# A graph network with an eigenvector stage: z's term as a one-row product on TensorE, the tangents' sum on GpSimd, the basis copy on ScalarE, and the reflection's scalars ahead of the copy of Y

## The chip, the cores and the metric

One NeuronCore of a Trainium2 chip runs the whole program in one launch. The metric is the device time of an execution in microseconds. Engines: TensorE (PE in the profile, its weight loads PEld), VectorE (DVE), ScalarE (ACT), GpSimd (POOL) and SyncE (SP), each with its own in-order queue; they meet at semaphores only.

## The reference

The input is x, 64 x 128 x 128 in float32, and a sparse matrix `adj`, 128 x 128. Four layers follow, each as `x = layernorm(x + layer(x))`: layer 0 a graph convolution with two batch norms, layer 2 graph attention over 256 edges with four heads, layer 3 two graph convolutions and then windowed LSTMs of 1 to 4 steps. The one that matters here is layer 1:

```
deg = sum(A, 0) + sum(A, 1) - diag(A)
L_norm = d_inv_sqrt[:, None] * (diag(deg) - A) * d_inv_sqrt[None, :]
_, U = eigh(L_norm)
agg = einsum('mn,bnd->bmd', U.T, features)
h = relu(agg @ W1 + b1);  out = h @ W2 + b2
return einsum('nm,bmd->bnd', U, out)
```

All eigenvectors of a 128 x 128 matrix are needed, with their signs fixed, before layer 1 can begin.

## The kernel before, in words

The program is written out without loops on the chip; every engine's queue is written by its own function, in its own order. After the loads and the graph's matrices (to 39 us of the span) comes the eigenvector stage (39 to about 458 us), and then layers 1, 2 and 3 and the final norm.

In the eigenvector stage three things run interleaved.

- *Sixteen Jacobi turns* (`SWEEPS`) that improve a basis V of eigenvectors, kept as it is (`v_nat`) and transposed (`v_t`). A turn, in the order of its chain: W = L V on TensorE (`pe_w`, L507), copied by ScalarE (L1069); the off-diagonal products (`pe_off`, L511, L512) and the diagonals (GpSimd's product L1406, then `pe_diagonals`, L516, L517); VectorE's differences (L1626); ScalarE's square, sign and absolute value (L1077 to L1079); the sum (L1631) and its root on ScalarE (`act_hyp`, L1083); the tangents on VectorE (`dve_tangents`: sum L1637, reciprocal L1638, product L1639); a norm on ScalarE (L1087 to L1089) and the scaled B on VectorE (L1643 to L1645); B transposed (L521); X (L1649); Y and the first product with V (L525 to L527); the copy of Y on ScalarE (`act_y`, L1094); Y squared (L531, L532) and its copies (L1098, L1099); the polynomial on VectorE (L1653 to L1664) with one more product (L537); and the new V and V transposed (`pe_v`, L542, L543), copied by VectorE (`dve_v`, L1669) and ScalarE (`act_vt`, L1104). In turns 9, 11, 13 and 15 (`POLISHED`) a correction of V with three more products and a second pair of copies follows.
- *Sixty-three reflection steps* that bring the matrix to tridiagonal form, one column each (what they keep fixes the signs of the eigenvectors at the end); four steps go with a turn and a fifth with a polished one (`steps_of`), none with turn 8, where the first 32 are put together to a basis (`removal_turn`). A step: VectorE computes the next column as a row c (L1713) and its sum of squares (L1720); ScalarE scales and takes a root (`act_vector`, L1115, L1117); GpSimd makes the scalars (`pool_scalars`: sign L1390, live L1392, sigma L1394, the changed leading entry L1397, half the square L1399). Meanwhile TensorE has made the matrix of the step before (L571, L573, L574 into `h_mat`), ScalarE copies it (`act_matrix`, L1124, L1125), TensorE multiplies out a row of it and y (`pe_rows`, L562, L563) and ScalarE copies the row (`act_row`, L1132). VectorE then forms z = sigma * row + y (L1689), the reciprocal (L1691), v scaled (L1692, which SyncE stores with a small DMA), a reduction of their product (L1696), w (L1698), a helper row (L1702) and the next c. w and v scaled go to TensorE for the rank-two change (`pe_rank`).
- *Layer 0 as side work* (`beside`, `behind_rank`): the slot number is the reflection step. Steps 0 to 20 carry the aggregation (L460) and hidden products (L467, saved by ScalarE, L1003), 22 to 40 the output products (L473, L474) and their statistics, 43 to 63 the transposition back (L481), the addition (L1578), the layer-norm statistics (L1581, L1585) and the writing of x.

`jacobi_turn(i)` exists once for each engine and lists these pieces by hand: four steps h0 to h3 and the turn's operations between them. Each engine waits where it stands, so a piece that is not ready holds all that is listed behind it.

## Time and profile before

| what | value |
|---|---|
| median of three runs | 1087.52 us (1086.25 to 1088.42) |
| the profiled execution | 1086.33 us, span 1084.5 us |
| TensorE busy in the span | 933.4 us (86%), 4093 instructions |
| VectorE busy | 659.7 us (61%), 2237 instructions |
| ScalarE busy | 569.2 us (52%), 1460 instructions |
| GpSimd busy | 158.8 us (15%), 390 instructions |
| mean granted TensorE clock | 0.881 |

The span is what the profiler saw from the first to the last instruction; the execution's own time is 1.8 us longer. Busy shares are means over stages with different limits. The chain of waits (the work that ended last, followed back) is what tells for a stretch which engine was late. A piece of it is the part of an instruction that lies on the chain, so it can be shorter than the instruction.

### The profile page before, as it was taken

To read this page: it belongs to the slowest core of one execution; us is meant where nothing else is said; L and a number is where in the kernel's file an instruction comes from. 1 tells how busy PE (TensorE), PEld (TensorE's weight loads), DVE (VectorE), ACT (ScalarE), POOL (GpSimd) and SP (SyncE) were. 2 spreads that over 40 slices of the span, in tenths; PEclk is the share of its full clock that TensorE was granted. 3 is DMA by queue.
4 is the path that set the end of the run, shared out by engine and by line. 5 is a ranking of instruction groups with operands and counts; after the bars stand their busy time and mean duration, and the time that the engine had idled before them with its cause. 6 is when DMAs were issued, how large, how long until landed. Compare 5 with 4: busy or idle time off the path is not lost.

```text
span 1084.5 us, 13522 instructions
## 1 busy us (share of the span) xinstructions
PE 933.4 (86%) x4093; PEld 631.0 (58%) x4093; DVE 659.7 (61%) x2237; ACT 569.2 (52%) x1460; POOL 158.8 (15%) x390
## 2 busy tenths in 40 slices
PE   4788867878866676699999999999999998899995
PEld 3555545545555565466788877886444465554443
DVE  4667676654757788357635598533544455553686
ACT  0555543754534665338655345534965565664456
POOL 0122222311322222100000000000011111110055
PEclk9699985977956555589999999999999999999998
DMA  9100000000000000000000000000000000000014
GB/s 261 32 1 1 1 1 0 1 1 1 1 1 1 1 1 1 1 1 1 1 1 1 1 2 1 2 1 1 1 1 0 0 1 1 1 0 1 0 40 116
DMA packets 14328, 12.99 MB, mean 12 GB/s; under 512 B 897, under 2 KB 11057, under 8 KB 14257
## 3 DMA queue, kind: packets, MB, share of 16 engines
q1 hardware_dynamic: 14018, 11.98, 3.9%
q8 instruction: 33, 0.54, 0.2%
q14 instruction: 39, 0.31, 0.1%
q10 hardware_dynamic: 238, 0.16, 0.1%
HBM read 7.89 MB, written 4.19 MB: 11 GB/s over the span
## 4 chain that ended last, share of the span: by engine, by line
PE 71%; DVE 18%; ACT 5%; issue 3%; POOL 1%; DMA 0%; DVEq 0%; SPq 0%; POOLq 0%; ACTq 0%
PE bank L884 15%; PE bank L908 9%; PE bank L805 3%; PE bank L750 3%; PE bank L740 3%; PE bank L764 3%; PE bank L795 3%; PE bank L467 2%; PE bank L573 2%; PE bank L704 2%; PE bank L460 1%; PE bank L715 1%; PE bank L871 1%; PE bank L813 1%; PE bank L863 1%
## 5 line engine op out<-in xcount | busy, mean ns | idle before, releaser
L1330 ACT ACTIVATE hid_t<-bank,gate_b 128x512 f32<-128x512 f32 (+1 forms) x252 | 150.8, 631 | 67.8 <-PE bank L908 66.7
L908 PE MATMUL bank<-ms,w_t 128*128 128x512 f32 (+1 forms) x288 | 112.9, 536 | 6.8 <-DVE ms L2062 6.8
L884 PE MATMUL bank<-hid_t,w_t 128*128 128x336 f32 (+1 forms) x296 | 106.4, 506 | 1.1 <-DVE x L2066 1.1
L1422 POOL COPY hid_t<-feat_t 128x1008 f32<-128x1008 f32 (+1 forms) x12 | 27.9, 2328 | 499.3 <-DVE feat_t L2058 499.3
L884 PE MATMUL bank<-feat_t,w_t 128*128 128x512 f32 x208 | 93.1, 603 | 0.0
L908 PEld LDWEIGHTS bank<-ms,w_t 128*128 128x128 f32 x288 | 54.6, 193 | 56.5 <-issue 34.3
L884 PEld LDWEIGHTS bank<-hid_t,w_t 128*128 128x128 f32 x296 | 56.2, 191 | 46.0 <-issue 26.2
L1124 ACT ACTIVATE hs<-bank,con 128x1 f32<-128x1 f32 x62 | 16.2, 261 | 102.3 <-PE bank L574 102.3
L1337 ACT ACTIVATE hid_t<-hid_t 128x512 f32<-128x512 f32 (+1 forms) x72 | 41.8, 580 | 52.3 <-DVE hid_t L2044 27.6
L884 PEld LDWEIGHTS bank<-feat_t,w_t 128*128 128x128 f32 x208 | 39.2, 189 | 50.9 <-issue 46.7
L982 ACT ACTIVATE x<-x,perm 128x128 f32<-128x128 f32 x128 | 52.3, 482 | 2.6 <-DVE perm L1461 2.6
L2044 DVE TENSOR_TENSOR hid_t<-hid_t 128x512 f32<-128x512 f32 (+1 forms) x36 | 42.3, 1175 | 17.0 <-ACT hid_t L1330 16.9
L467 PE MATMUL bank<-at,w_t 128*128 128x512 f32 x64 | 36.2, 649 | 15.1 <-ACT hid_t L1003 15.1
L2047 DVE TENSOR_TENSOR hid_t<-hid_t 128x512 f32<-128x512 f32 (+1 forms) x36 | 21.9, 609 | 42.5 <-ACT hid_t L1330 42.5
L1891 DVE TENSOR_TENSOR ht<-ht,bank 128x512 f32<-128x512 f32 x32 | 21.9, 688 | 40.4 <-ACT ht L1258 40.4
L2058 DVE TENSOR_TENSOR feat_t<-hid_t 128x512 f32<-128x512 f32 (+1 forms) x36 | 25.9, 720 | 26.4 <-ACT hid_t L1337 26.4
L1429 POOL TENSOR_SCALAR x<-x,perm 128x128 f32<-128x128 f32 x32 | 29.3, 928 | 75.8 <-DVE perm L2091 75.8
L562 PE MATMUL bank<-u_t,con 128*1 128x127 f32 (+62 forms) x126 | 24.6, 286 | 17.7 <-ACT u_t L1125 10.8
L2062 DVE TENSOR_TENSOR ms<-hid_t 128x512 f32<-128x512 f32 (+1 forms) x36 | 22.0, 611 | 25.2 <-ACT hid_t L1337 25.2
L2049 DVE TENSOR_TENSOR hid_t<-hid_t 128x512 f32<-128x512 f32 (+1 forms) x36 | 21.9, 610 | 24.9 <-ACT hid_t L1330 24.9
L1258 ACT ACTIVATE ht<-bank 128x512 f32<-128x512 f32 x32 | 19.1, 597 | 33.6 <-PE bank L750 33.6
L1394 POOL TENSOR_SCALAR hs<-hs 1x1 f32<-1x1 f32 x64 | 21.5, 336 | 88.6 <-ACT hs L1117 88.4
(443 smaller groups left out, 2166.7 us busy)
## 6 DMA issues: line engine op xcount, KB each, us to landing
out<-x SPq DMA_DIRECT2D x16, 256.0 KB, 2.6
con<-in_constants SPq DMA_DIRECT2D x1, 449.0 KB, 3.2
hid_t<-in_L_gnn_W SPq DMA_DIRECT2D x2, 128.0 KB, 3.7
e_int<-in_L_gnn_src ACTq DMA_DIRECT2D x1, 128.0 KB
l_w<-in_L_gnn_W SPq DMA_DIRECT2D x2, 64.0 KB
wg<-in_L_gnn_Wg SPq DMA_DIRECT2D x2, 64.0 KB
adj_n<-in_adj SPq DMA_DIRECT2D x1, 64.0 KB, 3.7
hid_t<-in_L_gnn_W_lin SPq DMA_DIRECT2D x1, 64.0 KB, 3.3
```

Of the source, the lines that this page charges most:

```text
L467: mm(l0_mid[k][:, :], w_t[:, WB_W1 + k, :], at[n % 2][:, :, :], start=True, stop=True).then_inc(s["l0_hid"], 1)
L740: d = mm(bank[2 + k][:, b * E:(b + 1) * E], xs[t % 2][:, 2 * k + b, :], w_t[:, WB_LIN:WB_LIN + 2, :], start=True, stop=True)
L750: d = mm(bank[4 + k][:, b * E:(b + 1) * E], z_lin[t % 2][:, 2 * k + b, :], sum_st[:, :], start=True, stop=True)
L764: d = mm(bank[6 + half][:, 0:E], head_strip[:, P - HEADS - r:2 * P - HEADS - r], rhs[:, b * E:(b + 1) * E], start=(r == 0), stop=(r == P - ...
L795: mm(bank[2 * (t % 2) + c][:, :], dst_st[:, c * P:(c + 1) * P], z_val[:, t * TB:(t + 1) * TB, :], start=True, stop=True).then_inc(s["l2v_v ...
L805: d = mm(bank[4][:, b * P:(b + 1) * P], w[c][:, b, :], src_s[:, c, :], start=(c == 0), stop=(c == EC - 1))
L884: return mm(bank[4 * u + BANK_OF[g]][:, 0:w], w_t[:, WB_IH + 4 * (it.p - 1) + g, :], lstm_x(n), start=True, stop=(it.k == 0))
L908: mm(bank[4 * u + BANK_OF[g]][:, 0:w], w_t[:, WB_HH + 4 * (it.p - 1) + g, :], lstm_h_of(it.chain)[:, 0:w], start=False, stop=True).then_in ...
L982: d = f(x[:, t * TB + b, :], x[:, t * TB + b, :], ACT.Identity, scale=ln_rs[:, t, b:b + 1], bias=ln_shift[:, t, b:b + 1])
L1330: f(dst[:, 0:w], bank[4 * u + BANK_OF[g]][:, 0:w], ACT.Tanh if g == G_G else ACT.Sigmoid, bias=gate_b[:, 4 * (it.p - 1) + g:4 * (it.p - 1) ...
L1337: f(th[n % 4][:, 0:w], cc[it.chain % 2][:, 0:w], ACT.Tanh).then_inc(s["lstm_tanh"], 1)
L2044: tt(c[:, 0:w], gi[u][:, 0:w], gg[u][:, 0:w], ALU.mult).then_inc(s["lstm_c"], 1)
```

## The change

Four edits in the eigenvector stage, and a renaming.

- z's term: the product y now stays open in its bank (`stop=False`), and a new function `pe_z(h)` adds sigma times the row by a product of one row with a 1x1 weight. It waits for the row (`h_a_row`) and for sigma (`h_sigma`) and signals `h_rows`. VectorE's L1689 is gone; the reduction and w read the bank directly. `pe_z` stands ahead of `beside` in each step: behind W in step 0, behind the transposition of B in step 2, behind Y squared in step 3.
- The tangents' sum: `jabs + jhyp` is now done by GpSimd (`pool_den`) behind the scalars of the turn's second step; VectorE waits for `j_den`.
- The basis copy: the copy of V into `v_nat` moves from VectorE (`dve_v`) to ScalarE, inside `act_vt`, ahead of the copy of V transposed.
- Scalars: in step 2 ScalarE runs `act_vector` ahead of `act_y` and no longer behind it.
- The semaphores `fin_var`, `fin_std` and `fin_scale` are replaced by counts on `ln_var`, `ln_std` and `ln_scale`; the waits stay the same.

```diff
-                mm(h_y[:, k:P], c_col, a_sb[:, k:P], start=True, stop=True).then_inc(s["h_rows"], 1)
+                mm(h_y[:, k:P], c_col, a_sb[:, k:P], start=True, stop=False)
+
+            def pe_z(h):
+                if h is None or h == HALF - 1:
+                    return
+                k = h + 1
+                pe.wait_ge(s["h_a_row"], h + 1)
+                pe.wait_ge(s["h_sigma"], h + 1)
+                mm(h_y[:, k:P], scalar(h, SIGMA), a_row[h % 2][:, k:P], start=False, stop=True).then_inc(s["h_rows"], 1)
...
                 pe_rows(h0)
                 pe_w(i)
+                pe_z(h0)
                 beside(h0)
                 pe_off(i)
                 pe_rank(h0)
                 pe_diagonals(i)
                 behind_rank(h0)
                 pe_rows(h1)
+                pe_z(h1)
                 beside(h1)
                 pe_rank(h1)
                 behind_rank(h1)
                 pe_rows(h2)
                 pe_turn(i)
+                pe_z(h2)
                 beside(h2)
                 pe_rank(h2)
                 pe_y(i)
                 behind_rank(h2)
                 pe_rows(h3)
                 pe_y2(i)
+                pe_z(h3)
                 beside(h3)
                 pe_f(i)
...
+                act.wait_ge(s["j_v"], i + before + polished + 1)
+                t = f(v_nat, j_v, ACT.Copy)
+                if polished or i not in POLISHED:
+                    t.then_inc(s["j_v_sb"], 1)
+                else:
+                    t.then_inc(s["j_m"], 1)
                 act.wait_ge(s["j_vt"]
...
                 act_row(h2)
                 beside(h2)
-                act_matrix(h2)
+                act_step(h2)
                 act_y(i)
-                if h2 is not None:
-                    act_vector(h2 + 1)
...
+            def pool_den(i):
+                pool.wait_ge(s["j_hyp"], i + 1)
+                pool.tensor_tensor(jt, jabs, jhyp, ALU.add).then_inc(s["j_den"], 1)
+
             pool_scalars(0)
             for i in range(SWEEPS):
                 pool_vw(i)
-                for h in steps_of(i):
+                for n, h in enumerate(steps_of(i)):
+                    if n == 1:
+                        pool_den(i)
                     if h is not None and h != STEPS_BEFORE - 1 and h + 1 < HALF:
                         pool_scalars(h + 1)
...
             def dve_tangents(i):
-                dve.wait_ge(s["j_hyp"], i + 1)
-                link(tt(jt, jabs, jhyp, ALU.add))
+                dve.wait_ge(s["j_den"], i + 1)
                 link(dve.reciprocal(jhyp, jt))
                 tt(jt, jos, jhyp, ALU.mult).then_inc(s["j_t"], 1)
...
                 if h < HALF - 1:
-                    dve.wait_ge(s["h_rows"], h + 1)
                     dve.wait_ge(s["h_a_row"], h + 1)
-                    dve.wait_ge(s["h_sigma"], h + 1)
-                    link(stt(z_row[:, k:P], a_row[h % 2][:, k:P], scalar(h, SIGMA), h_y[:, k:P], ALU.mult, ALU.add))
                 dve.wait_ge(s["h_half"], h + 1)
                 link(dve.reciprocal(scalar(h, INV), scalar(h, HALFSQ)))
                 ts(pv[:, k:P], v[:, k:P], scalar(h, INV), None, ALU.mult).then_inc(s["h_pv"], 1)
                 if h == HALF - 1:
                     return
                 dve.wait_ge(s["h_pv"], h + 1)
-                link(dve.tensor_tensor_reduce(e_vec[:, k:P], pv[:, k:P], z_row[:, k:P], 0.5, 0.0, ALU.mult, ALU.add,
+                dve.wait_ge(s["h_rows"], h + 1)
+                link(dve.tensor_tensor_reduce(e_vec[:, k:P], pv[:, k:P], h_y[:, k:P], 0.5, 0.0, ALU.mult, ALU.add,
                                               hs[0:1, 16:17]))
-                stt(w_row[:, k:P], v[:, k:P], hs[0:1, 16:17], z_row[:, k:P], ALU.mult, ALU.subtract).then_inc(s["h_w"], 1)
+                stt(w_row[:, k:P], v[:, k:P], hs[0:1, 16:17], h_y[:, k:P], ALU.mult, ALU.subtract).then_inc(s["h_w"], 1)
...
-                dve_v(i, 0)
```

## Rows read from the trace of the kernel before

**Rows 1.** The page's slices of 27.1 us each, granted clock; windows: busy us by engine, PEclk, DMA share, GB/s

```profile
PEclk9699985977956555589999999999999999999998
...
400.00:440.00 40.00, 26.66 (x120) 22.17 (x120) 30.96 (x159) 22.62 (x88) 9.11 (x33) 0.54 0.00 1
```

**Rows 2.** Sources by line: ns min/median/max, first and last start, forms

```profile
L563 PE MATMUL bank<-u_t,hs x126: 229/269/420, 39.4 to 435.5; 128*1 128x127 f32 x2, 128*1 128x126 f32 x2, 128*1 128x125 f32 x2, 128*1 128x124 f32 x2
...
L1637 DVE TENSOR_TENSOR perm<-perm x16: 271/273/291, 49.0 to 426.3; 128x128 f32<-128x128 f32 x16
...
L1669 DVE COPY av<-bank x20: 260/284/292, 64.5 to 443.3; 128x128 f32<-128x128 f32 x20
...
L1689 DVE SCALAR_TENSOR_TENSOR rows<-rows,hs,bank x63: 262/298/335, 40.0 to 437.6; 1x127 f32<-1x127 f32 x1, 1x126 f32<-1x126 f32 x1, 1x125 f32<-1x125 f32 x1, 1x124 f32<-1x124 f32 x1
```

**Rows 3.** Chain of waits in the stage: start us, us, what; first and last pieces

```profile
39.58 0.42 PE bank L563 x2
...
148.47 0.23 DVE rows L1689
...
150.19 0.21 DVE perm L1637
...
426.34 0.21 DVE perm L1637
...
435.56 0.21 PE bank L563 x2
...
437.60 0.28 DVE rows L1689
```

**Rows 4.** Instructions in order of time: start us, us; the end of turn 14

```profile
415.51 0.28 ACT L1104 ACTIVATE av<-bank 128x128 f32<-128x128 f32 x1 [0.37 <-PE bank L543]
...
416.44 0.28 DVE L1669 COPY av<-bank 128x128 f32<-128x128 f32 x1
...
416.78 0.80 PE L507 MATMUL bank<-av,lap 128*128 128x128 f32 x2 [0.77 <-DVE av L1669]
```

**Rows 5.** Instructions in order of time, step 3 of turn 14

```profile
411.84 0.27 DVE L1689 SCALAR_TENSOR_TENSOR rows<-rows,hs,bank 1x69 f32<-1x69 f32 x1
...
413.20 0.69 PE L573 MATMUL bank<-rows,src_st 1*128 1x69 f32 x2 [0.43 <-DVE rows L1698]
```

**Rows 6.** Instructions in order of time, step 1 of turn 6

```profile
195.43 1.12 PE L473 MATMUL bank<-ht,w_t 128*128 128x512 f32 x2
...
195.98 0.23 ACT L1132 ACTIVATE rows<-bank 1x102 f32<-1x102 f32 x1
...
198.02 0.46 PE L573 MATMUL bank<-rows,seg 1*128 1x102 f32 x2 [0.41 <-DVE rows L1698]
```

**Rows 7.** Instructions in order of time, step 3 of turn 6

```profile
208.46 0.30 DVE L1660 SCALAR_TENSOR_TENSOR diag_mat<-perm,diag_mat 128x128 f32<-128x128 f32 x1
...
209.29 0.15 DVE L1691 RECIPROCAL hs<-hs 1x1 f32<-1x1 f32 x1 [0.19 <-POOL hs L1399]
```

**Rows 8.** Instructions in order of time, step 1 of turn 3

```profile
124.93 1.10 PE L467 MATMUL bank<-at,w_t 128*128 128x512 f32 x2 [1.39 <-ACT hid_t L1003]
```

**Rows 9.** Instructions in order of time, step 1 of turn 0

```profile
46.67 2.08 PE L460 MATMUL bank<-ahat_t,x 128*128 128x128 f32 x8
...
46.85 0.25 ACT L1132 ACTIVATE rows<-bank 1x126 f32<-1x126 f32 x1
```

**Rows 10.** Instructions in order of time, step 0 of turn 14

```profile
391.75 0.45 POOL L1406 TENSOR_TENSOR wv<-av,wv 128x128 f32<-128x128 f32 x1 [1.51 <-ACT wv L1069]
...
391.77 0.52 DVE L1702 SCALAR_TENSOR_TENSOR rows<-rows,tmp 1x71 f32<-1x71 f32 x1
```

**Rows 11.** Instructions in order of time, step 2 of turn 14

```profile
404.83 0.28 DVE L1645 TENSOR_SCALAR src_b<-perm,js 128x128 f32<-128x128 f32 x1
...
406.38 0.28 DVE L1702 SCALAR_TENSOR_TENSOR rows<-rows,seg 1x69 f32<-1x69 f32 x1
...
406.59 0.33 DVE L1649 TENSOR_SCALAR src_b<-bank,js 128x128 f32<-128x128 f32 x1
```

## The prediction: what the change does to the time

> **What bounds the kernel now.** I read the table of slices on the page first, then the busy times of a stretch, then the chain of waits through the eigenvector stage, and last the instructions in order of time, turn by turn. The change touches only the stage from 39 to about 458 us; what comes after has TensorE at full speed and nearly always busy, and the edits there only rename semaphores. In the slices the reader is to see TensorE's granted clock: 0.5 to 0.9 in most slices of the stage, 0.9 and 1.0 after it; from 400 to 440 us it is 0.54, so mostly the lower level of 1.2 GHz, with TensorE busy 26.7 of 40 us and VectorE 31.0 [rows 1]. No engine is full there. The stage is two recurrences, the reflections (63 steps) and the Jacobi turns (16), on five in-order queues, with layer 0 as side work, and what counts is which queue is late at each step.
>
> The chain says it by place. The old term of z (L1689 on VectorE) is on it at 16 of 63 steps, the tangents' sum (L1637) at 12 of 16 turns, the copy of V (L1669) 8 times of 20; the product beside them, L563 on TensorE, is on it at 23 steps [rows 3]. So VectorE is late in the quiet turn 4 and from 350 us on, where the layer-0 additions and statistics are on it; TensorE, or ScalarE in front of it, is late in turns 0 to 3 and at the long side products of turns 5 to 10.
>
> **z's term moved to TensorE.** Removed: one VectorE instruction of 0.298 us median [rows 2] and its link wait of some 0.03. Where it is on the chain it gives its piece: 16 pieces from 148.47 to 437.60 us [rows 3] sum to 4.4 us, with the links 4.9. Added: a product with a 1x1 weight and one row of at most 127 columns, two passes as every float32 product here. The trace has no such operation. The nearest row is L563, as many columns with 128 rows under them: on the chain it takes 0.42 at the lower clock with 127 columns and 0.21 near the end with 65 [rows 3]. The upper bound is L573, one row under 128 weight columns, 0.69 for both passes with its restart [rows 5]; the lower is nothing, where TensorE idles anyway. I take 0.25 for the place in the queue and 0.45 until VectorE can read. VectorE needs z only at the reduction, some 0.5 us after the reciprocal, so where row and sigma are early the product is covered, and where it is not, VectorE waits 0.1 to 0.2.
>
> It costs in the TensorE queue. It is put ahead of the side work, and it waits for the row (ScalarE, L1132) and for sigma; side work, rank products and diagonals stand behind it.
> - At step 0 of a turn it follows W, at step 3 Y squared. In turns 1 to 3 ScalarE covers it: TensorE idles 1.39 us before the hidden product, waiting for a saved tile [rows 8]. Of the 23 places where L563 is on the chain I count 8 so covered; the other 15 cost 0.25 each, 3.8 us.
> - At step 2 it stands between the transposition of B and the side work, both on the chain at 7 turns: 1.8 us.
> - At step 1 the row is late, as ScalarE makes it behind the three operations on the differences. In turn 6 the side product L473 starts at 195.43, while the row is done at 196.21, so it starts at 196.5 instead. L573 started at 198.02 after 0.41 us of idling for w [rows 6]; 1.05 later it starts about 0.65 late, ScalarE's next matrix with it, and what VectorE saved in this step is lost. The same holds in turns 7, 9 and 10: four times 0.5, 2.0 us. In turn 0 L460 starts at 46.67 and the row ends at 47.10 [rows 9]: 0.43 of waiting and the product, 0.8 us, all on the chain.
>
> VectorE now reads the bank twice. Same form, same size class: L1689, which reads a bank, took 0.27, L1702 from SBUF alone 0.28 [rows 5, 11]; L1649, from a bank, 0.33, where L1645, from SBUF, took 0.28 [rows 11]. So between -0.01 and +0.05 an instruction; I take 0, by the row of the same form, and keep 0.05.
>
> The Trainium skill says otherwise, in "VectorE: DVE Perf Modes", section "The TRN2 errata": a VectorE operation from PSUM has 120 fixed cycles where one from SBUF has 58. At the page's 0.96 GHz that would be 0.065 us an instruction, 0.13 a step, by my estimate some 8 us over 62 steps if all were on the chain; L1689 against L1702 does not agree with it.
>
> **Tangents' sum to GpSimd.** L1637 takes 0.273 us, 16 times [rows 2]; 12 pieces from 150.19 to 426.34 us [rows 3] sum to 2.6, with links 3.0. GpSimd needs about 0.45, as for L1406, same size and type [rows 10]. It waits for the root, behind it are only the scalars of the next step, which have nothing to do yet. The reflection's five VectorE instructions (over 1.2 us) cover it except in turn 8, which has none: there 0.45 and two semaphores replace 0.3, a loss of 0.2. While L1406 ran, L1702 took 0.52 for its usual 0.28 [rows 10, 11], so 0.24 can come back at each turn; its lower end is 0, as the reciprocal that now runs beside the sum has one input. I take 0.1 a turn: gain 3.0 - 1.2 - 0.2 = 1.6 us.
>
> **Copy of V to ScalarE, ahead of that of V transposed.** The 8 pieces of the chain, from 164.78 to 416.44 us (the last one's instruction is in [rows 4]), sum to 1.9 us, with restarts 2.2. At the ends of the late turns there is more: in turn 14 V transposed is copied at 415.51, but V only at 416.44, behind the statistics, and W's product starts at 416.78 after 0.77 us idle [rows 4]. With both on ScalarE, each 0.25 to 0.28 and overlapping by some 0.1, W starts near 416.05: 0.7 gained, so 0.4 beyond the copy, at four such ends, 1.6. Sum 3.8 us. ScalarE pays 0.2 ahead of the row of the next step; where W came at once anyhow (turn 6) W is 0.1 later, which I leave inside the rounding.
>
> **Scalars ahead of the copy of Y.** On ScalarE square and root of the next step ran behind the copy of Y, and in turn 6 the reciprocal waited for GpSimd until 209.29, with L1660 done at 208.76 [rows 7]. Now L1660 ends last: 0.5 us, in turn 6 and likewise turn 9, 1.0 us. Elsewhere VectorE's own order is later. The copy of Y is not delayed: it waits for three products behind the rank, longer than the scalars take.
>
> **Sum.** Gains 4.9 + 1.6 + 3.8 + 1.0 = 11.3; costs 3.8 + 1.8 + 2.0 + 0.8 = 8.4; net -2.9 us. The profiled execution took 1086.33 us (span 1084.5), which gives 1083.4; the median of the three runs is 1.2 us above it, so 1084.6 on that footing. By stretch: turn 0 about +1, turns 1 to 3 none, turn 4 about -1, turns 5 to 10 none, turns 11 to 15 about -3.
>
> **Rivals.**
> - *TensorE's queue decides (slower).* Place: the new product ahead of the side work. Price: 0.25 each, 62 times, 15.5 us, and holds of 2.8. It decides from the point where more than (11.3 - 2.8) / 0.25 = 34 products are on the path instead of the 22 counted. For it: 23 steps have L563 on the chain, and removing VectorE work makes TensorE the later one. Against: TensorE idles 0.4 to 0.8 us ahead of W and of the rank products [rows 4, 5]. With 45 on the path: +2.8, 1090.3. Chance 0.16.
> - *Hidden on both sides.* Each engine relieved was late by less than the next one: in turn 14 L573 had idled only 0.43 us for w [rows 5], and the product z takes 0.25 of it. If half of the gains are so cut: -5.6 + 5.6 (the costs that lie on the same steps shrink too), 1087.5. Chance 0.18.
> - *The bank read costs.* VectorE holds a bank longer than SBUF at each read: 0.05 twice a step at the 31 or so steps where VectorE is late, +3.1, 1087.6. L1649 speaks for it, L1689 against it [rows 5, 11]. Chance 0.05. (The skill's page on VectorE, section "The TRN2 errata", would price these same steps at 4 us, an estimate.)
> - *The holds cost nothing and the late turns give fully.* Without the 2.0 of turns 6 to 10 and the 1.8 at step 2: -6.7, 1080.8. For it: VectorE was last there too, so half of the delay is slack. Chance 0.13.
> - *The clock moves.* Between turns 4 and 11 the granted clock changes often [rows 1]; an L473 to L474 stretch costs twice as much at the lower level. Shifted turns can meet another level at one or two places, 1 to 2 us either way, the sign open. This widens every case and has no chance of its own.
>
> **Numbers.** My forecast, a gain of 1.5 to 5 us, has 0.48. It is likeliest at 1084.5. Its own range is 1082.2 to 1086.0; from 1080.3 to 1089.5 about 2 in 10 are left out. 0.2% is 2.2 us, about what a measurement of this kernel can tell from no change; faster means under 1085.3. Faster: 0.40 of the forecast's 0.48, the 0.13, and 0.03 of the hidden case: 0.56. Slower: the first rival and a little of the third: 0.18. Same: 0.26.
>
> **What would show it.** VectorE: no L1689, and the reciprocal straight behind L1660 or behind GpSimd's last scalar; a wait of VectorE for TensorE ahead of the reduction under 0.2 us at most steps. If that wait is over 0.4, the term of z is mis-sized. TensorE: the new product some 0.2 us in the queue at the upper level and 0.3 at the lower; L460 in turn 0 some 0.8 later against L563's end, L473 of step 1 in turn 6 some 1 us. W's product in turn 14 within 0.3 us of the copy of V transposed. The distance between successive matrices of differences (L1626) shorter by 0.5 to 1 us from turn 11 on and unchanged in turns 1 to 3. It is wrong if turns 1 to 3 grow, or if turns 11 to 15 shrink by less than 1.5 us together, or if the stage's granted clock moves by more than 0.03.

## The result: 1090.45 us, slower by 0.44%

| | before | changed |
|---|---|---|
| median, us | 1086.8 (1085.38 to 1088.53, 20 executions) | 1090.45 (1086.5 to 1101.04, 20 executions) |
| ratio | | 1.0044 (1.003 to 1.0059) |
| profiled execution / its span, us | 1086.33 / 1084.5 | 1091.17 / 1089.1 |
| granted clock of the profiled execution | 0.881 | 0.877 |

I had forecast 1084.5, and 0.56 for faster. The time lies outside the wider of my two ranges (1080.3 to 1089.5) by 1 us, and on the other side of the kernel before. One execution of `no_z` below took 1963 us: it stands apart from all others, and its range, ratio and low time leave it out, while its median of five counts it.

In the changed kernel the lines are: L563 and L564 the row products, L572 the new one-row product, L580, L582 and L583 the rank products, L1152 the row on ScalarE, L1118 and L1124 the copies of V and of V transposed, L1702 the reciprocal, L1708 the reduction, L1714 the last of the reflection's vectors; the side work is L461, L474, L475, L482. The clock slices of the profile after and one of its windows, in the form of [rows 1]:

```profile
PEclk9599985895956555589999999999999999999998
...
400.00:440.00 40.00, 28.60 (x128) 22.12 (x128) 29.93 (x156) 23.03 (x89) 10.42 (x35) 0.50 0.01 1
```

TensorE is busy 28.6 of 40 us where it was 26.7, VectorE 29.9 where it was 31.0: work moved, but the time did not fall. The distances between the matrices of differences (L1626 before, L1650 after) say where. After the start of turn 0 they give: turn 0 +3.3 us, turns 1 to 4 +0.4, turns 5 to 10 +4.4, turns 11 to 15 -3.4. The late turns are as forecast (-3), turn 0 (+1) and turns 5 to 10 (none) are not. The 4.4 hide more: turn 7 alone is 3.6 us shorter (18.1 for 21.7), and TensorE's lower level is gone from it (0 us for 10.2); the five others grew by 8.1.

The new product's line, with what TensorE idled for ahead of it and who waited for it:

```profile
L572 PE MATMUL bank<-rows,hs x126: 226/262/415, 39.4 to 441.5; 1*1 1x127 f32 x2, 1*1 1x126 f32 x2, 1*1 1x125 f32 x2, 1*1 1x124 f32 x2
its engine sat idle before it (us, times) until:
  ACT rows L1152: 21.5, 30
...
  POOL hs L1412: 0.9, 2
who waited for it (us, times):
  DVE rows L1708: 5.8, 13
```

So at 30 of 63 steps TensorE stands still for the row, 21.5 us in all, where I had named five. In the chain of waits (start, us, what) L572 now has 36 pieces, which sum to 12.2 us; the first and the last:

```profile
39.49 0.51 PE bank L572 x2
...
436.09 0.32 PE bank L572 x2
```

I had counted 22 places at 0.25, 5.6 us. VectorE's L1708 has no more than 5.8 us of waiting for it in all.

### The profile page after: what moved, and what is told of

It reads as the page before. It is cut to its first block, busy times and chain, and to the rows that moved or that the text cites. A ratio compares the mean times of both kernels' runs of the same rounds, so it can differ in the third digit from the quotient of the medians.

```text
span 1089.1 us, 13759 instructions
## 1 busy us (share of the span) xinstructions
PE 962.8 (88%) x4219; PEld 639.7 (59%) x4219; DVE 632.1 (58%) x2138; ACT 572.5 (53%) x1480; POOL 165.3 (15%) x406
## 4 chain that ended last, share of the span: by engine, by line
PE 76%; DVE 14%; ACT 6%; issue 3%; POOL 1%; ACTq 0%; DMA 0%; DVEq 0%; POOLq 0%
PE bank L898 15%; PE bank L922 9%; PE bank L582 3%; PE bank L819 3%; PE bank L754 3%; PE bank L764 3%; PE bank L778 3%; PE bank L809 3%; PE bank L468 2%; PE bank L461 2%; PE bank L583 2%; PE bank L474 2%; PE bank L718 1%; PE bank L729 1%; PE bank L475 1%
## 5 line engine op out<-in xcount | busy, mean ns | idle before, releaser
L2056 DVE TENSOR_TENSOR hid_t<-hid_t 128x512 f32<-128x512 f32 (+1 forms) x36 | 21.9, 609 | 42.2 <-ACT hid_t L1348 42.2
L468 PE MATMUL bank<-at,w_t 128*128 128x512 f32 x64 | 36.7, 656 | 10.2 <-ACT hid_t L1017 10.2
L1900 DVE TENSOR_TENSOR ht<-ht,bank 128x512 f32<-128x512 f32 x32 | 21.9, 688 | 40.3 <-ACT ht L1276 40.3
L2067 DVE TENSOR_TENSOR feat_t<-hid_t 128x512 f32<-128x512 f32 (+1 forms) x36 | 26.0, 722 | 26.7 <-ACT hid_t L1355 26.7
L563 PE MATMUL bank<-u_t,con 128*1 128x127 f32 (+62 forms) x126 | 25.0, 290 | 17.9 <-ACT u_t L1145 11.0
L1276 ACT ACTIVATE ht<-bank 128x512 f32<-128x512 f32 x32 | 19.1, 597 | 33.6 <-PE bank L764 33.6
L2058 DVE TENSOR_TENSOR hid_t<-hid_t 128x512 f32<-128x512 f32 (+1 forms) x36 | 21.9, 609 | 24.8 <-ACT hid_t L1348 24.8
```

The lines of the kernel that those rows point to most:

```text
L468: mm(l0_mid[k][:, :], w_t[:, WB_W1 + k, :], at[n % 2][:, :, :], start=True, stop=True).then_inc(s["l0_hid"], 1)
```

## Experiments

Two theories of mine stood against each other. *Queue*: the product and its two waits stand in front of TensorE's other work at more steps than the 22 counted. *VectorE*: z comes late to the reduction. A third, the *clock*, says that a longer or emptier stage draws more time at TensorE's lower level. "Low time" below is 2 x (1 - granted clock) x span of an execution, which is the time at the lower level, as the clock is at 1.2 or 2.4 GHz: the mean is 258 to 260 us for the kernel before and 269 for the changed one. Among the 20 executions of the changed kernel the time rises by 0.28 us per us of low time (1086.5 to 1088.5 at clock 0.883, 1101 at 0.864), among those of the kernel before by 0.20 to 0.26 in four sets. "By ratio" is the ratio times 1086.8.

### Which edit

`no_z` is the changed kernel with z as VectorE's operation again:

```diff
-                mm(h_y[:, k:P], c_col, a_sb[:, k:P], start=True, stop=False)
+                mm(h_y[:, k:P], c_col, a_sb[:, k:P], start=True, stop=True).then_inc(s["h_rows"], 1)
...
-                pe_z(h0)
...
+                    link(stt(z_row[:, k:P], a_row[h % 2][:, k:P], scalar(h, SIGMA), h_y[:, k:P], ALU.mult, ALU.add))
```

> The changed kernel with z's term back on VectorE; the other three edits stay. Theory of the queue (the one-row product and its waits ahead of the side work cost more than VectorE's instruction): turns 1 to 3 fall back by 0.1 us a turn, turn 0 by 1 to 3 us, the late turns keep the gain of the basis copy, so about 1083 to 1085 us, 2 to 4 under the kernel before. Theory of the clock (what the edits do to the work is small, the granted clock of the stage decides): the time stays between 1086 and 1092, spread over several us from execution to execution, and follows the clock.

Measured 1075.87 (1073.66 to 1077.03), ratio 0.9897 (0.9881 to 0.9913), clock 0.891: faster than either theory had said. `z_only` is the other way about, the kernel before with z in the bank and nothing else:

> The kernel before with z's term on TensorE and nothing else. Queue: at least the whole loss, 1091 to 1093. Clock: anything from 1087 to 1095, with a wide spread, lower clock with longer time at 0.25 to 0.3 us for each us more at the lower level.

Measured 1100.2 (1099.71 to 1101.04), ratio 1.0123 (1.011 to 1.0136), clock 0.873. The three other edits gain 11.2 us by ratio, z in the bank loses 16.0 on top of them and 13.4 alone; I had 6.4 and 3.5. So most of the loss does not need the other three edits: the new product is on the chain of waits in `z_only` at 33 places, 11.6 us, against 36 and 12.2 in the changed kernel.

`z2_first` moves z of step 2 ahead of the transposition of B; `fill_turn` puts dead products ahead of the wait for B:

```diff
-                pe_turn(i)
                 pe_z(h2)
+                pe_turn(i)
```
```diff
             def pe_turn(i):
+                for _ in range((6 if i > 11 else 4 if i > 8 else 0)):
+                    mm(j_bt, ident, ident, start=True, stop=True)
```

> The changed kernel with the product z of step 2 ahead of the transposition of B instead of behind it. In the late turns VectorE waits 0.65 us for it ahead of the reduction of step 2; that wait should go (row and sigma are there 1.5 us earlier). Queue: 4 late turns and turns 4, 5 gain 0.3 to 0.7 each, so 2 to 3 us under the changed kernel, about 1088. Clock: the wait goes, the total may not follow.

Measured 1084.23 (1081.56 to 1095.26), ratio 0.9994 (0.997 to 1.0018): 5.4 us back by ratio, more than the 2 to 3 expected. This step had the longest wait ahead of the reduction (below). The mean low time is 260 us for 269, so some 2 of the 5.4 can be the clock, by the slopes.

> The changed kernel with idle time of TensorE filled: 4 (turns 9 to 11) or 6 (turns 12 to 15) extra 128x128 products of the identity with itself, results never read, ahead of the wait for B. The output is unchanged. Clock: if what TensorE does between its waits sets the granted clock, the stretch from 340 to 440 us (0.5 now) rises, and each turn there gets shorter by 2 us or more, the total by 5 to 10 us. Queue: nothing gained, at most 1 us lost where the fill is not done when B is.

Measured 1084.31 (1077.07 to 1090.67), ratio 0.9968 (0.9946 to 0.999), mean low time 239 us instead of 269: dead work in TensorE's idle time gains 8.3 us by ratio.

### Waits, product, or both

`hold_only` is `no_z` with only TensorE's two waits at z's places; `product_only` is `no_z` with one more one-row product (weight zero) ahead of y's and no wait; `hold_product` has both at z's places, into a part of a bank that nobody reads, while VectorE still computes z:

```diff
# hold_only                                  # hold_product: the same, and
+                pe.wait_ge(s["h_a_row"], h + 1)
+                pe.wait_ge(s["h_sigma"], h + 1)
+                mm(h_a[:, k:P], scalar(h, SIGMA), a_row[h % 2][:, k:P], start=True, stop=True)
# product_only
+                mm(h_y[:, k:P], con[0:1, C_TAIL:C_TAIL + 1], con[0:1, k:P], start=True, stop=False)
-                mm(h_y[:, k:P], c_col, a_sb[:, k:P], start=True, stop=True).then_inc(s["h_rows"], 1)
+                mm(h_y[:, k:P], c_col, a_sb[:, k:P], start=False, stop=True).then_inc(s["h_rows"], 1)
```

> z stays VectorE's operation, as in the version with the other three edits alone (1075.9). Added are only TensorE's two waits, for the row and for sigma, ahead of the side work at every step; no product. Changed kernel: 1090.5, so the term of z is 14.6 us on this footing. If the holds make it: 1085 to 1090. If the product's own time in TensorE's queue makes it: 1076 to 1079 (the 2.8 that I had put on holds is the most). If it is VectorE's wait for z ahead of the reduction: 1076 to 1079 too, as VectorE waits for nothing new here. If it is the clock that goes with the distance between products: low level within 5 us of the version without z for a time within 2 us of it. My own guess: holds 5 to 8, 1081 to 1084.

> z stays VectorE's operation; added is only one more product of one row (its weight is a zero, so that y is unchanged) in the bank ahead of y's, at every step; no new wait. If the product's own time in the queue makes the 14.6 us: 1085 to 1090 (62 products at 0.2 to 0.25). If it is the holds or VectorE's wait: 1077 to 1080, the product being mostly covered (15 places of 0.25 at most, 3.8). My own guess: 1079 to 1081.

> z stays VectorE's operation (1075.9 without anything on TensorE). TensorE gets at z's places both of the changed kernel's waits and the same one-row product, but into a part of another bank that nobody reads, so y is not later by it and VectorE waits for nothing new. What this lacks of the changed kernel's 1090.5 is VectorE's wait for z ahead of the reduction, less the VectorE instruction removed. Holds alone gave 1076.5 to 1078, the product ahead of y 1082.9. If holds and product add up in TensorE's queue: 1083 to 1087, and VectorE's wait is worth the rest. If they interact (a hold places the product where it is no longer covered): 1088 to 1092. If most of what the product did ahead of y was y's delay in front of VectorE, and little the queue: 1077 to 1081, and VectorE's wait is worth most of the 14.6. My own guess: 1080 to 1084.

| on the footing of `no_z` | median, us | ratio | by ratio | mean low time, us |
|---|---|---|---|---|
| `no_z` | 1075.87 | 0.9897 (0.9881 to 0.9913) | 0 | 242 |
| `hold_only` | 1076.5 | 0.9922 (0.9897 to 0.9946) | +2.7 | 244 |
| `product_only` | 1082.89 | 0.9985 (0.9965 to 1.0005) | +9.6 | 244 |
| `hold_product` | 1094.92 | 1.0079 (1.0065 to 1.0092) | +19.8 | 277 |
| changed | 1090.45 | 1.0044 (1.003 to 1.0059) | +16.0 | 269 |

The holds cost what the prediction had put on them (2.8), and not the 5 to 8 that I expected before this run. The product costs 9.6 instead of 5.6, with only 2 us more of low time. It does not stand at z's place there: y comes 0.42 us later in the mean (0.62 us behind L563 for 0.20), and VectorE waits for y at 13 places, 16.9 us, where it did at 4 places, 4.2 us, in `no_z`. Together they cost 7.5 more than their sum (3 to 12, by the intervals of the four ratios), and with them comes 33 us more of low time, worth 7 to 9 us by the slopes above. The changed kernel is 3.8 us below `hold_product`: that is what the removal of VectorE's instruction is worth, with its wait for z paid. `hold_product` is far above my guess (1080 to 1084). In it and in `product_only` VectorE has all its work for z, and still the added product is on the chain at 37 places (13.0 us) and at 32 (10.5).

The step of turn 6 that the prediction had worked out [rows 6] shows the hold. The changed kernel, in order of time:

```profile
198.54 0.34 PE L564 MATMUL bank<-u_t,hs 128*1 128x102 f32 x2
199.36 0.23 ACT L1152 ACTIVATE rows<-bank 1x102 f32<-1x102 f32 x1
199.64 0.33 PE L572 MATMUL bank<-rows,hs 1*1 1x102 f32 x2 [0.76 <-ACT rows L1152]
199.90 1.12 PE L474 MATMUL bank<-ht,w_t 128*128 128x512 f32 x2
...
202.01 0.46 PE L582 MATMUL bank<-rows,seg 1*128 1x102 f32 x2
```

`no_z` at the same place:

```profile
192.67 0.34 PE L564 MATMUL bank<-u_t,hs 128*1 128x102 f32 x2
192.93 1.12 PE L474 MATMUL bank<-ht,w_t 128*128 128x512 f32 x2
193.90 1.02 PE L475 MATMUL bank<-ms,w_t 128*128 128x512 f32 x2
194.75 0.36 PE L572 MATMUL bank<-u_t,con 128*128 128x102 f32 x2
195.47 0.46 PE L574 MATMUL bank<-rows,seg 1*128 1x102 f32 x2 [0.36 <-DVE rows L1699]
```

And `hold_only`:

```profile
194.99 0.34 PE L564 MATMUL bank<-u_t,hs 128*1 128x102 f32 x2
196.09 1.13 PE L474 MATMUL bank<-ht,w_t 128*128 128x512 f32 x2 [0.76 <-ACT rows L1150]
...
198.20 0.46 PE L580 MATMUL bank<-rows,seg 1*128 1x102 f32 x2
```

And `product_only`, where the one-row product stands ahead of y's:

```profile
198.72 0.33 PE L563 MATMUL bank<-u_t,con 128*1 128x102 f32 x2
198.99 0.33 PE L564 MATMUL bank<-con 1*1 1x102 f32 x2
...
201.70 0.46 PE L575 MATMUL bank<-rows,seg 1*128 1x102 f32 x2
```

From y's product to the first rank product that needs w it is 2.80 us without z, 3.21 with the wait alone, 3.47 with the product too. The idle 0.36 us for w in `no_z` is the slack: the hold of 0.84 uses it up and comes out 0.41 late, and from there the product's 0.26 counts in full. From L563, the product ahead of it in all of them, it is 2.98 in `no_z`, 2.98 in `product_only` (the slack hides the product), 3.38 in `hold_only`, and 3.64 in `hold_product` and the changed kernel. So at this step a wait eats the slack that would have hidden the product.

How far this goes is read from the distances between the L563 of one step and of the next, 62 of them, in the profiles of `no_z`, `hold_only`, `product_only` and `hold_product`. (That of `product_only` is one of its four longer executions of twelve, 1087.72 us.) At nine steps of turns 6 to 10 all four have the higher level throughout: there the holds cost 1.5 us, the product 0.75 and both 4.25, so 2.0 beyond the sum. At the 13 such steps of turns 0 to 4 the product costs 2.6 us ahead of y, and product and holds 0.3 at z's place. At the 13 steps where all four have the lower level both cost 0.4 more than the sum. Over these 35 steps that comes to 0.1 beyond the sum; the other 4.7 of the 4.8 us that the profiles show lie in the 27 steps at which the level is not the same in all four, or changes. So eaten slack is shown, at nine steps with 2.0 us, but it is not shown to make the 7.5: there slack and level are not told apart.

The same reading for the whole of z's term: the changed kernel's profile is 19.8 us longer over these 62 distances than that of `no_z` (the medians differ by 14.6). Of this 5.7 us lie in the 41 steps at which both have one level all through, the same in both, and 14.1 in the 21 others, which have 35 us more of low time, worth 7 to 10 by the slopes. The queue and the clock each have a large part; the split is an estimate.

`z_behind` puts z's product behind the side work:

```diff
-                pe_z(h0)
                 beside(h0)
+                pe_z(h0)
```

> The changed kernel with z's product behind the side work instead of ahead of it, at every step: no hold of the side work, but VectorE's reduction waits for the side work too. If the holds make the loss: 1079 to 1083. If VectorE's wait ahead of the reduction makes it: slower than the changed kernel, over 1095, as the wait of 0.65 us at step 2 grows by a side product of 0.5 to 1.5. If the product's own time makes it: 1088 to 1092, unchanged. My own guess: between, 1086 to 1098, slow in the turns with long side products (5 to 10) and faster in turn 0.

Measured 1116.06 (1112.2 to 1124.09), ratio 1.0282 (1.0249 to 1.0315). Turns 1 to 4 are 31.2, 30.9, 29.8 and 25.1 us long instead of 25.5, 25.5, 24.5 and 23.5, as the reduction waits for a side product: it waits for z at 48 steps, 80.1 us in all. The place ahead of the side work was the better of the two, and the loss is larger than I had guessed (1086 to 1098).

### By stretch

z goes back to VectorE in turn 0 alone, in turns 5 to 11 alone, or stays in the bank at 13 steps only that looked shorter in the changed kernel's trace:

```diff
+def z_in_bank(h):
+    return h > 3                     # z_not_turn0
+    return h < 20 or h > 45          # z_not_middle
+    return h in (4, 8, 12, 16, 40, 42, 44, 45, 46, 49, 53, 58, 62)   # z_chosen
```

> The changed kernel with z back on VectorE in the four steps of turn 0 alone. My prediction priced turn 0 at 0.8 us; the profiles show it 4.4 us longer with z in the bank than without, and the run with holds alone 2.2 longer. If the profile's turn 0 is what every execution pays: 1085 to 1087. If the holds of turn 0 are 0.8 and the rest was the clock's draw in the profiled execution: 1089 to 1090.

Measured 1088.82 (1086.5 to 1093.92), ratio 1.002 (1.0008 to 1.0032): turn 0 is worth 2.6 us by ratio, not 0.8, and not the 4.4 by which the end of turn 0 comes later in the profile of the changed kernel than in that of `no_z`.

> The changed kernel with z back on VectorE in turns 5 to 11 alone (the long side products). The prediction priced the holds and products there at 3.8 to 5 against gains of about the same size, so 1089 to 1091 by it. The profiles give 9.7 us more in these turns with z in the bank: if that is what every execution pays, 1080 to 1083. If most of it was a few stretches at the lower clock level in one execution: 1086 to 1088. My own guess: 1082 to 1085.

Measured 1078.07 (1074.27 to 1084.18), ratio 0.9927 (0.99 to 0.9954): turns 5 to 11 carry 12.7 of the 16.0 us. Windows from turn 4's matrix of differences to turn 11's, and from there to the stage's end, in the columns of [rows 1]. Changed kernel:

```profile
149.70:316.30 166.60, 139.25 (x601) 89.15 (x600) 92.23 (x364) 81.22 (x291) 43.14 (x141) 0.75 0.00 1
316.30:443.60 127.30, 99.36 (x449) 76.76 (x449) 90.70 (x467) 71.85 (x274) 33.19 (x112) 0.53 0.00 1
```

`no_z`:

```profile
145.00:301.80 156.80, 123.76 (x551) 82.43 (x550) 99.18 (x388) 81.62 (x291) 43.66 (x141) 0.77 0.00 1
301.80:425.80 124.00, 86.18 (x405) 71.54 (x406) 96.81 (x488) 71.14 (x274) 33.44 (x112) 0.57 0.00 1
```

`z_not_middle`:

```profile
146.00:302.70 156.70, 125.89 (x557) 83.76 (x556) 98.39 (x385) 81.71 (x291) 43.68 (x141) 0.76 0.00 1
302.70:427.00 124.30, 94.04 (x441) 73.49 (x441) 91.08 (x470) 71.24 (x274) 33.53 (x112) 0.56 0.00 1
```

In the middle TensorE is busy 84% of the time with z in the bank (139.25 of 166.6) and 79% without; the stretch is 9.8 us longer than in `no_z` and 9.9 longer than in `z_not_middle`, at a clock of 0.75 for 0.77 and 0.76 (83 us of low time for 72 and 76). In the late window of `z_not_middle` the 17 products of turns 12 to 15 cost 0.3 us (124.3 against 124.0, one profile each). Some of the middle is still the clock. The same side product at step 1 of turn 9, changed kernel:

```profile
266.59 0.32 PE L572 MATMUL bank<-rows,hs 1*1 1x94 f32 x2 [0.79 <-ACT rows L1152]
266.84 1.39 PE L474 MATMUL bank<-ht,w_t 128*128 128x512 f32 x2
268.02 1.91 PE L475 MATMUL bank<-ms,w_t 128*128 128x512 f32 x2
269.73 0.57 PE L580 MATMUL bank<-u_t,con 128*128 128x94 f32 x2
```

`no_z`:

```profile
256.23 1.12 PE L474 MATMUL bank<-ht,w_t 128*128 128x512 f32 x2
257.19 1.02 PE L475 MATMUL bank<-ms,w_t 128*128 128x512 f32 x2
258.05 0.35 PE L572 MATMUL bank<-u_t,con 128*128 128x94 f32 x2
```

The side pair takes 2.89 us to L580 instead of 1.82, at the lower level, after TensorE had idled 0.79. A second such stretch follows at 274.4, together 2.3 of the 5.2 us by which this turn is longer than in `no_z`.

> z in the bank only in 13 steps at which the profile of the changed kernel has a shorter step than the version without it (step 0 of turns 1 to 4 and of turn 12, and eight steps of turns 10 to 16), on VectorE in the others; 1075.9 without any. If the mechanism is place by place (VectorE late: gain of 0.1 to 0.35; TensorE late: loss of 0.3 to 0.5): 1072 to 1074, the sum of the differences being 3.4. If a gain in one step is given back in the next, because TensorE is only just behind: 1075 to 1077. If any product in this queue costs: over 1078.

Measured 1076.48 (1075.46 to 1080.01), ratio 0.9908 (0.9895 to 0.9921), against 0.9897 without any: nothing gained, where place by place I had added up 3.4 us. I had put this outcome down beforehand to a gain that the next step gives back. The runs do not show that: the mean low time is 256 us here and 242 in `no_z`, which alone is worth 3 to 4 us by the slopes.

### The other three edits, one at a time

Each was added alone to the kernel before.

> The kernel before with the copy of V on ScalarE alone. By the prediction's term: 3.8 us gained, 1083. The other three edits together gave 11.7, nearly twice the sum of their terms of 6.4. If the copy's ends of late turns are the mis-sized term: 1078 to 1081. If all three add up as predicted and the rest is the clock: 1082 to 1084 with 10 to 20 us less at the lower level.

> The kernel before with the tangents' sum on GpSimd alone. By the prediction's term: 1.6 us gained, 1085.5. If GpSimd's 0.45 us is covered fully and the slowing of VectorE beside it is nothing: 3.0, 1084. If it is a loss (two semaphores for one instruction where VectorE comes to it late): 1087 to 1089.

> The kernel before with the scalars of the next step ahead of the copy of Y alone. By the prediction's term: 1.0 us gained, 1086. If they are late at more steps than the two that I counted, as the slice of steps 2 to 3 in the comparison of the traces suggests (0.3 us shorter in each of turns 1 to 3): 2 to 4 gained, 1083 to 1085.

Measured: the copy 1078.47 (ratio 0.992, 0.9906 to 0.9934), the tangents' sum 1080.87 (0.9953, 0.9941 to 0.9966), the scalars 1083.0 (0.9968, 0.9956 to 0.998). That is 8.7, 5.1 and 3.5 us by ratio, where I had 3.8, 1.6 and 1.0; together they give 11.2, so 6.1 of their sum of 17.3 overlaps. All three are above their terms. With the sum or the scalars alone the distance from turn 7's matrix of differences to turn 8's is 18.8 us instead of 21.7: in it the level was low for 3.4 us and not for 10.2. So 2.9 us of each goes with the clock's level, which either moves, and it can be gained once; the other 3.2 of the overlap are not explained. The copy gains in turns 11 to 14: in its profile they are 9.3 us shorter, and of 103.8 us 77 are at the lower level, where it was 103 of 113.0.

### The clock by itself

`no_z_fill` has the dead products of `fill_turn` in `no_z`; `fill_more` has four of them in turns 5 and 6 as well, and three at step 1 of turns 11 to 15:

```diff
+                if i > 10:
+                    pe.wait_ge(s["h_a_row"], h1 + 1)
+                for _ in range(3 if i > 10 else 0):
+                    mm(h_mat, ident, ident, start=True, stop=True)
```

> The version with the other three edits alone (1075.9, 1071.5 the span, 222 us at the lower clock level within the stage) with the same filling products as in the run before that gained 6.2 us on the changed kernel: 4 dead products ahead of the wait for B in turns 9 to 11, 6 in turns 12 to 15. If the clock is a cause of its own, with 0.2 to 0.35 us for each us at the lower level: low-level time under 195 us and 1066 to 1071. If what filling gained was only the loss of z given back: 1075 to 1077.

Measured 1068.85 (1066.48 to 1070.39), ratio 0.983 (0.9815 to 0.9846), mean low time 214 us.

> The version with the three other edits and the filling products in turns 9 to 15 (1068.9), with 4 more ahead of the wait for B in turns 5 and 6, and 3 more at step 1 of turns 11 to 15, where TensorE waits 1.7 to 2.6 us for w. None of these is in front of work that is due. If the clock level is a cause of its own (0.2 to 0.35 us for each us at the lower level, level low for 208 us in the stage now): 185 us low or less, and 1060 to 1066. If the level no longer answers to such filling: 1068 to 1070. If they delay the products behind them: slower than 1070.

Measured 1065.87 (1063.23 to 1067.65), ratio 0.9803 (0.9789 to 0.9817), mean low time 211 us: the fastest version, 2% below the kernel before. The 23 dead products more take 2.9 us off `no_z_fill`, but the intervals of the two ratios touch and the low time hardly moves, so this last part is not shown to be the clock. Its slices, against [rows 1], are higher in the ninth, the twelfth and the fifteenth (and in the second and the eighteenth, lower in the third):

```profile
PEclk9789985987966575599999999999999999999998
```

Dead work gains 7.3 us on `no_z` and 8.3 on the changed kernel, so the loss by z is 15.0 with the filling and 16.0 without. Filling and z add up: filling gains about the same with z in the bank and without, and does not get z's loss back.

## Why the prediction was wrong

**The step that failed** is the term of the one-row product's place in TensorE's queue: "the other 15 cost 0.25 each, 3.8 us", and 1.8 at step 2. I counted its places by where L563 was on the chain of the kernel before [rows 3], as if a product put in could cost only where a product was late already. Put in, it is on the chain 36 times in the changed kernel, with 12.2 us (0.34 each), instead of 22 times with 5.6. It is not the work taken from VectorE that adds the places. With VectorE's z still there they are 32 (`product_only`) and 37 (`hold_product`), with nothing but z moved 33 (`z_only`); and in `no_z`, with the three other edits, the old product y is on the chain at 25 places, for 23 before. The product and its waits make their own places: they use up the slack that a step had, as at step 1 of turn 6.

**The second step that failed** is "1 to 2 us either way" for the clock. z in the bank brings 27 us more of low time than `no_z` has (269 for 242), 6 to 8 us by the slopes within one kernel.

My first rival said that TensorE's queue decides, from 34 places on; I gave it 0.16. The count of 36 bears it out, but not its reason, that relieving VectorE makes TensorE late. That its 1090.3 is so near the measured 1090.45 is luck: it had +9.2 for z's edit (14.1 less 4.9) where +16.0 was measured, and -6.4 for the three others where -11.2 was.

Term by term, with z's edit on top of the other three. The rows are differences between runs, so they add up by themselves; each holds what its change does to the clock:

| term, us | predicted | measured by ratio | from |
|---|---|---|---|
| product's place | +5.6 | +9.6, part of it y's delay | `product_only` |
| holds | +2.8 | +2.7 | `hold_only` |
| both together, beyond the sum | 0 | +7.5 | `hold_product` |
| VectorE's instruction, less its wait | -4.9 | -3.8 | changed against `hold_product` |
| three other edits | -6.4 | -11.2 | `no_z` |
| sum | -2.9 | +4.8 | |

- *Where mechanism and place were right:* at step 1 of turn 6 the side product starts 1.36 us after the row product instead of 0.27, and the rank product 0.61 later against it, for the "about 0.65" of the prediction [rows 6]. In turn 14 the copy of V transposed (L1124) ends at 421.02 and W's product starts at 421.18, within the 0.3 named, where it had idled 0.77 for the copy of V [rows 4]:

```profile
420.32 0.28 ACT L1118 ACTIVATE av<-bank 128x128 f32<-128x128 f32 x1
420.74 0.28 ACT L1124 ACTIVATE av<-bank 128x128 f32<-128x128 f32 x1
...
421.18 0.80 PE L508 MATMUL bank<-av,lap 128*128 128x128 f32 x2
```

- *Holds:* the number of places was wrong, five for 30, but `hold_only` costs 2.7 us, so most of these waits are covered. Turn 0 was worth 2.6 us for z in all, against 0.8; in the trace the row ends the wait at 46.72 [rows 9]:

```profile
46.42 0.25 ACT L1152 ACTIVATE rows<-bank 1x126 f32<-1x126 f32 x1
46.72 0.58 PE L572 MATMUL bank<-rows,hs 1*1 1x126 f32 x2 [0.41 <-ACT rows L1152]
...
47.23 0.58 PE L461 MATMUL bank<-ahat_t,x 128*128 128x128 f32 x1
```

- *VectorE's wait ahead of the reduction* is under 0.05 at 46 of 63 steps and 0.2 or more at 12, among them 0.65 to 0.68 at step 2 of turns 12 to 15, where z stands behind the transposition of B. That is over the 0.4 that the prediction named as the sign of a mis-sized term: less the 0.33 of the removed instruction, about 0.3 us net is lost in each of these turns. `z2_first` got 5.4 us back from step 2 as a whole.
- *Late turns:* shorter by 3.4 us in the trace, for 3 forecast. The agreement is partly luck, as the three other edits gave more than their terms and z took more. *Turns 1 to 3* grew by 0.1 each, which the prediction had named as a sign of error, and it was a small one.
- *The clock's* 6 to 8 us are an estimate from a correlation; that dead work which raises the level gains time is shown by the filling. Which pattern of work makes the level fall is not settled: TensorE idled 0.79 us ahead of the low stretch of turn 9, but the kernel without z idles up to 1.47 in that turn and stays at the higher level.
- *The bank read* (third rival): the reduction from SBUF in the kernel before, by source, and the one from the bank after, each for the steps of one buffer:

```profile
L1696 DVE CUSTOM_DVE_ANT_0 rows<-e_row,rows x16: 216/248/568, 41.2 to 425.5; 1x127 f32<-1x127 f32 x1, 1x123 f32<-1x123 f32 x1, 1x119 f32<-1x119 f32 x1, 1x115 f32<-1x115 f32 x1
```
```profile
L1708 DVE CUSTOM_DVE_ANT_0 rows<-e_row,bank x16: 213/244/275, 40.2 to 430.1; 1x127 f32<-1x127 f32 x1, 1x123 f32<-1x123 f32 x1, 1x119 f32<-1x119 f32 x1, 1x115 f32<-1x115 f32 x1
```

  Medians of 0.248 and 0.244 us: this read of the bank costs nothing. The Trainium skill's "VectorE: DVE Perf Modes", section "The TRN2 errata", would have made it 0.065 us longer by my estimate; this pair does not agree with it either.
- *The tangents' sum* takes 0.452 us on GpSimd, as L1406 did [rows 10]. What took longer beside it was not the reciprocal but the scaling ahead of the reduction (L1703, usually 0.26): twice its time in turns 0 and 14, at most 0.05 more in the others:

```profile
403.78 0.54 DVE L1703 TENSOR_SCALAR e_row<-e_row,hs 1x71 f32<-1x71 f32 x1
403.81 0.45 POOL L1428 TENSOR_TENSOR perm<-perm 128x128 f32<-128x128 f32 x1 [2.24 <-ACT perm L1097]
```

## What to carry to other kernels

An instruction put into a queue costs at more places than those where the queue was late before. Read for every step how much slack the receiving engine has ahead of what it needs next, and set against it the instruction and each wait that comes with it; the places on the chain of before (22 here, 32 to 37 with the product in) leave out the steps that the instruction itself makes late. A wait and an instruction behind it are not priced apart by one run each (2.7 and 9.6 us alone, 19.8 together): the wait can eat the slack that would have hidden the instruction, and both can move the clock. Where the granted clock changes within the stage, compare two profiles step by step, first the steps at the same level. Run each edit of a bundle by itself: three good ones (-11.2) were hidden here by a fourth (+16.0).

## What the runs showed of the hardware that I had not expected

- TensorE's granted clock answers to dead products in its idle time: 36 and 59 of them took the mean low time from 242 to 214 and 211 us and the time down by 7.3 and 10.2 us by ratio, although nobody reads what they compute.
- The stretch from turn 7's matrix of differences to turn 8's goes with the level in all 18 profiles: it lasts 17.2 to 18.1 us where the level was low for 0 us (three profiles, the changed kernel's among them), 18.6 to 19.1 where it was low for 3.4 (eight), 21.3 to 21.8 for 6.8 (two), 21.6 to 21.9 for 10.2 (four), and 25.4 for 16.8 (`z_behind`). What decides between them is not shown.
- A product with a 1x1 weight is not cheaper in the queue than one with 128 rows under it: in `product_only`, where the two stand side by side, 0.262 us median for a pass of the one-row product and 0.267 for y's. Its weight load is shorter, 0.076 against 0.081 us.
